# A vision tower on one core: own orders and two token banks in the last two steps, unread products in TensorE's waits, and an earlier first half of the tree

## The reference

```
tokens: patches of 1, 2 and 4 pixels along Hilbert curves, 16 to a group
        -> 256 tokens x 64 at each level (levels 2 and 3 interpolated to 256)
h = concat(levels) @ Wf.T + bf                              # 16 x 256 x 192
h = h + attention(layernorm(h))                             # 12 heads of 16, causal, softmax
all_logits = layernorm(h) @ weights_in.T                    # 21 nodes
walk a binary tree for 10 steps by the sign of the logit at the current node (index clipped to 20)
out = h + sum over the path of gelu(logit) * weights_out[node]
```

## Time and profile before

| | us |
|---|---|
| runs | 365.19, 367.33, 373.09 (median 367.33) |
| profiled execution, its own time | 369.12 |
| its span, first to last instruction | 367.1 |
| mean granted clock of TensorE, share of full | 0.902 |
| busy: PE, DVE, ACT, POOL | 302.2, 230.2, 191.6, 189.3 |

### The profile page before, as it was taken

The page is one execution under the profiler, slowest core; times in us unless marked ns, Lnnn a source line. Parts: engine busy times, 40 slices in busy tenths (PEclk is TensorE's granted clock), DMA queues, the critical chain, the costliest instruction groups (busy, mean ns, idle before and its releaser), DMA issues.

```text
span 367.1 us, 8188 instructions
## 1 busy us (share of the span) xinstructions
PE 302.2 (82%) x2684; PEld 225.3 (61%) x2684; DVE 230.2 (63%) x1135; ACT 191.6 (52%) x394; POOL 189.3 (52%) x410
## 2 busy tenths in 40 slices
PE   1943259899768498999999999999999979799663
PEld 1931028857657375777777777776677657576463
DVE  3000013235565857898889888898988883767872
ACT  1301002334453365865776586568657644568681
POOL 4777710000001047766866686686668663455642
PEclk9975557999996989999999999999999976999868
DMA  7611100020056044343654367353435622000018
GB/s 194 204 25 20 20 7 3 19 63 0 7 125 127 1 96 73 97 120 81 88 110 100 79 89 122 89 83 104 106 81 89 120 90 44 1 4 2 3 54 289
DMA packets 27633, 27.80 MB, mean 76 GB/s; under 512 B 6850, under 2 KB 27328, under 8 KB 27592
## 3 DMA queue, kind: packets, MB, share of 16 engines
q1 hardware_dynamic: 24472, 25.00, 31.1%
q0 software_dynamic: 1184, 1.58, 1.7%
q10 hardware_dynamic: 1936, 0.72, 0.9%
HBM read 4.86 MB, written 3.15 MB: 22 GB/s over the span
## 4 chain that ended last, share of the span: by engine, by line
PE 75%; issue 8%; DVE 6%; ACT 3%; DMA 3%; SPq 2%; POOL 1%; DVEq 0%; POOLq 0%; ACTq 0%
PE bank L1129 8%; PE bank L1306 7%; PE bank L1360 6%; PE bank L1338 6%; PE bank L1251 4%; PE bank L1302 4%; PE bank L1342 3%; PE bank L1270 3%; PE bank L1285 3%; PE bank L1287 3%; PE bank L1259 3%; PE bank L1230 3%; PE bank L1363 3%; PE bank L1242 2%; SPq L303 2%
## 5 line engine op out<-in xcount | busy, mean ns | idle before, releaser
L849 DVE CUSTOM_DVE_ANT_0 C<-bank,MASKV 128x256 bf16<-128x256 f32 (+1 forms) x384 | 112.6, 351 | 30.4 <-PE bank L1306 23.5
L569 ACT ACTIVATE PT<-bank 128x512 f32<-128x512 f32 x144 | 80.7, 606 | 52.8 <-PE bank L1338 48.8
L376 POOL TENSOR_SCALAR_AFFINE_SELECT PT<-PT 128x256 f32<-128x256 f32 x144 | 66.4, 474 | 0.0
L354 POOL TENSOR_TENSOR PART<-RES,PART 128x256 bf16<-128x256 f32 (+1 forms) x31 | 28.0, 904 | 62.0 <-ACT PART L563 62.0
L1129 PE MATMUL bank<-X,OH 128*128 128x192 f32 x128 | 31.3, 390 | 28.1 <-issue 20.1
L1129 PEld LDWEIGHTS bank<-X,OH 128*128 128x128 f32 x128 | 26.5, 231 | 31.7 <-issue 23.6
L372 POOL TENSOR_TENSOR CARRY<-CARRY 1x1 f32<-1x1 f32 x96 | 17.6, 184 | 54.1 <-ACT PT L569 54.0
L767 DVE TENSOR_SCALAR OH<-IR,IOTA 128x1024 f32<-128x1024 int32 x8 | 5.8, 751 | 53.0 <-remote 38.1
L349 POOL DMA_INDIRECT G<-x,I x32 | 30.7, 960 | 9.8 <-issue 9.8
L849 DVE DVE_READ_ACCUMULATOR2_ANT MX<- 128x1 f32 x384 | 31.9, 83 | 0.0
L1360 PE MATMUL bank<-PT,VA 128*32 128x256 f32 x384 | 30.9, 392 | 0.1
(11 more groups left out here) (167 smaller groups left out, 643.2 us busy)
## 6 DMA issues: line engine op xcount, KB each, us to landing
QS<-PART SPq DMA_DIRECT2D x72, 96.0 KB, 3.8
KS<-PART SPq DMA_DIRECT2D x72, 96.0 KB, 3.6
out<-HT SPq DMA_DIRECT2D x7, 384.0 KB, 3.5
KSL<-PART SPq DMA_DIRECT2D x24, 96.0 KB, 3.2
QSL<-PART SPq DMA_DIRECT2D x24, 96.0 KB, 3.6
X<-x SPq DMA_DIRECT2D x8, 96.0 KB
G<-x,I POOLq DMA_INDIRECT x34
IR<-ix1r SPq DMA_DIRECT2D x1, 512.0 KB
```

Source lines behind the costliest of these rows:

```text
L376: pool.affine_select(out=e, in_=e, compare_op=ALU.is_ge, fill=0.0, base=0, pattern=[[0, n], [1, P]], channel_multiplier=-1).then_inc(cut_o ...
L569: nc.scalar.activation(PT[:, v, :], BANK[T_BANK[(SU * par + v) % 2]][:, :], ACT.Exp, scale=SCALE).then_inc(exp_ok, 1)
L849: ins = nc.vector.tensor_tensor_reduce(JUNK[:, n:n + keys], bank[:, j * keys:(j + 1) * keys], MASKV[:, S - keys:S], 1.0, LOWEST, ALU.add, ...
```

## The change

- TensorE multiplies constants (`WP` by itself, 128x192 float32) into a bank that is about to be overwritten, and nobody reads the result: 10 such products ahead of the first step's wait, 10 ahead of `max_t(first)`, 3 ahead of the wait for the maxima in `scores_t` unit 0 of images 13, 14 and 15, 5 ahead of the last `project`, 1 and 2 around `tokens_t(15)`, 1 in each of `output(1)` to `output(4)`.
- Steps 14 and 15 get an order of their own on TensorE, ScalarE and VectorE (`closing_step`), and `tokens_t` alternates between banks 7 and 6. `project(12)` and `project(13)`, which use bank 6, wait for the copies.
- In the tail the logits are scaled for A and B apart (GpSimd), GELU of A and its coefficients come sooner, the remainders of A stand ahead of B's walk on GpSimd, its low parts still behind it; the GELU table for C is loaded ahead of `logits_t(7)`; VectorE copies `tokens_t(15)`; `coefficients_t(0)` and `(1)` stand around `logits(7)`, and `output(0)` follows at once; outputs take six banks in turn; GpSimd's output adds wait until C's coefficients are done.

```diff
-        OUT_BANK = [2, 3, 4, 6]
+        OUT_BANK = [2, 3, 4, 6, 5, 7]
...
-            return BANK[MB if i < 2 * 4 else S_BANK[i % 2]]
+            return BANK[(MB, MA)[i % 2] if i < 2 * 4 else S_BANK[i % 2]]
... GpSimd, tail
+            scaled(ROWS_A)
             pool.wait_ge(lgd_ok, 2)
-            pool.tensor_tensor(SL[:, ROWS_AB, :], LG[:, ROWS_AB, 0:NODES],
...
+            scaled(ROWS_B)
             normalise(Image(0, B - 1))
...
+            remainders(1, ROWS_A)
             pool.wait_ge(gn_ok, 2)
...
             low_parts(1, ROWS_A)
+            remainders(2, ROWS_B)
             low_parts(2, ROWS_B)
...
+            pool.wait_ge(co_ok, 3)
... ScalarE
+            def closing_step(b, par):
+                d, q = b - 1, 2 * (b.off - B + 2)
+                exp(d, 1 - par, 0)
+                tokens_t(2 * q)
+                exp(d, 1 - par, 1)
+                exp(d, 1 - par, 2)
+                exp(d, 1 - par, 3)
+                tokens_t(2 * q + 1)
+                exp(d, 1 - par, 4)
+                exp(d, 1 - par, 5)
+                logits_t(q)
+                tokens_t(2 * q + 2)
+                tokens_t(2 * q + 3)
+                exp(d, 1 - par, 6)
+                exp(d, 1 - par, 7)
+                exp(d, 1 - par, 8)
+                logits_back(q)
+                maxima(b)
+                logits_t(q + 1)
+                logits_back(q + 1)
...
-            gelu(1, ROWS_AB)
+            gelu(1, ROWS_A)
             tokens_t(14)
+            gelu(2, ROWS_B)
             logits_t(6)
             nc.scalar.activation(WARM[:, 0:1], WARM[:, 1:2], ACT.Sqrt)
             high_parts(ROWS_A)
-            tokens_t(15)
+            middle_parts(ROWS_A)
             deviations(5, ROWS_C)
-            middle_parts(ROWS_A)
+            nc.scalar.activation(WARM[:, 0:1], WARM[:, 1:2], ACT.Gelu)
             logits_t(7)
+            coefficients_t(0)
             high_parts(ROWS_B)
+            coefficients_t(1)
+            middle_parts(ROWS_B)
             gelu(3, ROWS_C)
-            middle_parts(ROWS_B)
-            coefficients_t(0)
-            coefficients_t(1)
             coefficients_t(2)
... VectorE
+            def closing_step(b, par):
+                d = b - 1
+                row_max(b, par, 0)
+                row_max(b, par, 1)
+                row_max(b, par, 2)
+                row_max(b, par, 3)
+                if b.late:
+                    centre()
+                row_max(b, par, 4)
+                row_max(b, par, 5)
+                row_max(b, par, 6)
+                heads_by_row(b - 2)
+                row_max(b, par, 7)
+                row_max(b, par, 8)
+                residual(b - 2)
+                heads_by_token(d, False)
+                residual_statistics(b - 2)
+                heads_by_token(d, True)
+                over_sums(d)
...
             residual(before)
+            own_rstd(4, ROWS_AB)
             copy_logits(5)
-            own_rstd(4, ROWS_AB)
             heads_by_token(last, False)
             heads_by_token(last, True)
             over_sums(last)
+            coefficients(1, ROWS_A)
+            heads_by_row(last)
             residual_statistics(before)
-            heads_by_row(last)
-            coefficients(1, ROWS_A)
             residual(last)
...
             variances(ROWS_C)
+            tokens_t(15)
             copy_logits(6)
...
+            output(0)
             for k in range(NQ):
-                if ADDED[k] == "dve":
+                if ADDED[k] == "dve" and k:
... TensorE
+            def keep_busy(bank, count):
+
+                for _ in range(count):
+                    nc.tensor.matmul(bank[:, 0:D], WP[:, 0, 0:P], WP[:, 0, :], start=True, stop=True)
...
                 if v == 0:
+                    if b.off >= B - 3:
+                        keep_busy(bank, 3)
                     pe.wait_ge(m_in, b.count(16, 16))
...
+            def closing_step(b, par):
+                d, q = b - 1, 2 * (b.off - B + 2)
+                for w in range(2):
+                    pe.wait_ge(stacked[w][par], 6 * 16 * (b.off // 2 + 1))
+                scores(b, par, 0)
+                scores(b, par, 1)
+                scores_t(d, 1 - par, 0)
+                tokens_t(2 * q)
+                if b.late:
+                    centre()
...
+                scores_t(d, 1 - par, 2)
+                tokens_t(2 * q + 1)
+                scores_t(d, 1 - par, 3)
+                scores(b, par, 4)
...
+                scores_t(d, 1 - par, 8)
+                project(b - 2)
+                weighted(d, 1 - par, 1)
+                max_t(b)
+                logits(q + 1)
+                weighted(d, 1 - par, 2)
+                logits_back(q + 1)
...
+                keep_busy(BANK[S_BANK[0]], 10)
                 for w in range(2):
                     pe.wait_ge(stacked[w][0], 6 * 16)
...
                 pe.wait_ge(ht_ok, B)
+                keep_busy(BANK[T_BANK[0]], 10)
                 max_t(first)
...
             logits(6)
+            pe.wait_ge(exp_ok, last.count(SU, SU))
+            keep_busy(BANK[T_BANK[0]], 5)
             project(last)
             logits_back(6)
+            keep_busy(BANK[T_BANK[0]], 1)
             tokens_t(15)
-            logits(7)
-            logits_back(7)
+            keep_busy(BANK[T_BANK[0]], 2)
...
+            coefficients_t(0)
+            logits(7)
+            coefficients_t(1)
+            logits_back(7)
             pe.wait_ge(w6_ok, 4 + PARTS)
-            for k in range(NQ):
+            output(0)
+            for k in range(2, NQ):
                 coefficients_t(k)
-                if k:
-                    output(k - 1)
+                output(k - 1)
             output(NQ - 1)
```

More of the change, by code:

```diff
@@ L687, in _ @@
             first_step()
[L688 removed]
+            for n in range(1, B - 2):
                 step(Image(0, n), n % 2)
+            for n in range(B - 2, B):
+                closing_step(Image(0, n), n % 2)
             last = Image(0, B - 1)
             def gelu(u, rows):
[L692 removed]
+                act.wait_ge(*((sl_ok, u) if u < 3 else (slc_ok, 1)))
                 nc.scalar.activation(GE[:, rows, :], SL[:, rows, :], ACT.Gelu).then_inc(ge_ok, 1)
@@ L916, in step @@
                 row_max(b, par, 0)
-                if b.late:
-                    centre()
                 if has_old:
@@ L1003, in _ @@
             first_step()
-            for n in range(1, B):
+            for n in range(1, B - 2):
                 step(Image(0, n), n % 2)
+            for n in range(B - 2, B):
+                closing_step(Image(0, n), n % 2)
             last = Image(0, B - 1)
@@ L1109, in _ @@
             last_reach(ROWS_B)
-            coefficients(1, ROWS_B)
+            coefficients(2, ROWS_B)
             own_rstd(5, ROWS_C)
@@ L1430, in step @@
                     narrow(f)
-                if b.late:
-                    centre()
                 scores_t(d, 1 - par, 0)
-                if closing:
-                    tokens_t(2 * q)
                 scores(b, par, 2)
```

98 lines of the change are left out of this document (49 added, 49 removed).

## The result

The changed kernel took 354.80 us in the median of four runs (354.23 to 355.40), beside 367.88 us for the kernel before. The ratio is 0.9668 (95% interval 0.9611 to 0.9726): 3.3% faster. The forecast was 356.5 us. The profiled execution took 354.23 us, with a span of 352.5 us and a mean granted clock of 0.943 (0.902 before).

What follows compares the result with a forecast made beforehand. TensorE was taken as the bound through the kernel's middle, losing time in waits and at half clock. Terms -2.6 - 1.5 - 1.5 - 5.0 - 2.5 + 0.3 = -12.8 us from 369.1 gave 356.3, stated as 356.5; range 351.5 to 364.

Steps and rivals of the forecast that it cites:

- the case that it called likeliest: Whole kernel: the forecast itself, 356.5 us, given a chance of 0.60.
- Part 1: Ahead of the first step: ten products fill the 4.24 us wait and hold the clock up, -2.6 us.
- Part 2: Ahead of `max_t(first)`: ten products fill the 4.16 us wait and keep the work behind it at full clock, -1.5 us.
- Part 3: Step 15: new order and second bank remove idle time, three products counted as 0.98 us of work, -1.5 us.
- Part 4: Step 14: same new order, with the 9.29 us at half clock now at full clock, -5.0 us.
- The sign of failing that I had named: Step 14: the prediction fails if the clock there is a matter of chance in both kernels.
- Part 5: Tail: five products ahead of the last `project`, earlier A coefficients and `output(0)`, -2.5 us.
- Part 6: Remaining products, around `tokens_t(15)`, in four outputs and ahead of the last image's scores: cost +0.3 us.
- The clock did not fall in the last two steps: Rival, steps 14 and 15: the clock falls all the same, giving back 4.65 us, 361; chance 0.15.
- the first step gave what it should: Rival, first step: it gives nothing, giving back 4.1 us, 360.5; chance 0.08.
- no product overran: Rival, all products: they run at low clock and overrun their waits, +10.6 us, whole kernel 376; chance 0.05.
- The tail's order loses: Rival, tail: collisions and late GpSimd adds make it 0.5 us slower instead of 2.5 faster, 359.5; chance 0.12.

Runs made afterwards that it cites:

- e2: Kernel before plus only the two groups of ten unread products (ahead of the first step and of `max_t(first)`): 364.07 us, ratio 0.9926.
- e1: Changed kernel without any of the unread products; orders, banks and tail rearrangement stay: 358.34 us, ratio 0.9741.
- e8: Kernel before plus only the second token bank, old orders of steps 14 and 15, no products: 361.44 us, ratio 0.9830.
- e3: Kernel before plus the own orders of steps 14 and 15 and the two token banks, no products, old tail: 360.67 us, ratio 0.9817.
- e7: Changed kernel with one token bank instead of two in steps 14 and 15; orders and products stay: 357.30 us, ratio 0.9756.
- e10: Changed kernel with VectorE's adds of `output(0)` moved ahead of C's walk: 323.89 us, ratio 0.9704 to the kernel before on the same chip.
- e13: The changed kernel run once more, unaltered, on another chip: 322.79 us, ratio 0.9645 to the kernel before there.
- e6: Kernel before plus both groups of ten products, two token banks and own orders of steps 14 and 15; old tail: 356.78 us, ratio 0.9739.
- e9: Changed kernel with `heads_by_row(last)` put back ahead of A's coefficients on VectorE: 356.84 us, ratio 0.9742.
- e4: Changed kernel without the three products ahead of the last image's transposed scores: 354.77 us, ratio 0.9648.
- e11: Changed kernel without GpSimd's wait for C's coefficients ahead of its output adds: 324.99 us, ratio 0.9742 to the kernel before on the same chip.

## Why the prediction was right, by its own steps

The forecast of 356.5 us was 1.7 us too high, and the case that it called likeliest came true. But the sum's agreement is better than its terms'.

**Part 1** (-2.6): right, -2.98. The reason holds too: the first step lost nearly the 3.05 us that half clock had cost, and e2 shows it alone. VectorE didn't become the bound there: of its four waits of 2.93 us in all one of 0.49 us is left. So the gain went to the end of the estimate.

**Part 2** (-1.5): too high. With the tens the way to step 2 is 1.1 us shorter in the change and 0.8 in e2. I wrote that there was room for 1.6 us, just. There wasn't: in all profiles with the tens TensorE stands idle ahead of step 2's first scores, 0.33 us in the change and 0.61 in e2, where the kernel before has no idle time. The profile names no releaser for it; in the program the wait for the stacked queries and keys stands there.

**Part 3, step 15** (-1.5): mis-sized, -2.7. The step has 12.10 us, all of it busy by the stretch's row, so the 0.3 us of idle time that I allowed aren't there. The other error is the 12.04 us of work, which I took as fixed: in e1 the same matmuls are busy 11.28 us of 12.18, and the rest is a wait of 0.90 us for the maxima. The triple stands in this wait and adds nothing. I had seen that it would cost nothing there and added its 0.98 us all the same. e8 shows that 1.6 of the 2.7 us are the bank's and e3 that 1.1 are the orders'.

**Part 4, step 14** (-5.0): size right, -5.7; the reason not as written. I put the full clock down to the triples and the denser order. e1 has no triples and e8 neither, and the clock stands in both; e7 keeps waits of 0.79 us and it stands too. In the profiles of kernels without second bank and without new orders (before and e2) it fell, and in none of the twelve others. But e8 shows the same work and the same waits ahead of the place, so for the bank alone this can't be read as cause and effect. The text said that the clock here may differ between executions and that the spread of the runs comes from it. The granted clocks of the single executions bear that out for the kernel before, on the chips of e10 to e13: spans of 330.2 to 330.7 us have a mean clock of 0.962 to 0.964, spans of 332.5 to 333.8 us 0.944 to 0.950, and spans of 334.5 us and more 0.945 or less.

Only one execution of each kernel has a trace, but the mean clocks allow an estimate: the missing share, doubled, times the span is the time at half clock. In the profile of the kernel before, the stretches around the first step and behind the fall in step 14 have

```profile
109.00:132.00 23.00, 15.14 (x80) 12.64 (x81) 14.32 (x96) 9.73 (x21) 4.96 (x7) 0.78 0.29 58
309.10:367.10 58.00, 42.74 (x498) 32.82 (x490) 37.69 (x140) 34.52 (x69) 29.64 (x66) 0.88 0.17 56
```

which is 10 and 14 us at half clock, and the fall in step 14 is 10 more. On the chips of e10 to e13 the front runs at 1.00 in all four traces, so an execution of the kernel before should have about 34 us with that fall and 24 without. Of its 18 executions there, 4 have 24 to 25 us and 14 have 33 to 41. The 20 executions of e10 to e13, which all have both banks and the new orders, have 4 to 11. By this estimate the kernel before loses the clock in step 14 in most executions, the change in none, so step 14 in the two profiles is what most executions have. The sign of failing that I had named, chance in both kernels, didn't come. But what decides it is not shown: which of bank and orders keeps the clock up, and why it stands or falls behind equal work. For the bank alone the times give a hint only. e8's median is 4.6 us under that of before (6.2 by the ratio). At any clock the bank takes 1.6 us off step 15 (14.82 to 13.24) and 0.4 off step 14 (18.56 less half of the 9.29 us at half clock is 13.9, against 13.51). That leaves 2.6 to 4.2 us for the clock, in step 14 or elsewhere.

**Part 5, the tail** (-2.5): the term that was mis-sized most, about 0 by the profiles (33.54 us before, 33.40 after; e6 with the old tail 33.33). My -2.5 was +0.4 for the way to `project`, -1.2 for `project` itself and -1.7 for what comes behind it. Measured are +1.3, -0.9 and -0.5. The -0.9 are there in e3, e6 and e8 as well (end 18.50 us), whose tail is the old one: the last `project` runs at the full clock in them, too. What I counted on for `output(0)` was there: it starts 3.4 us sooner behind `project`. What went wrong is this:

- The way to the last `project` grew by 1.3 us, and A's coefficients, to which I gave 0.6, are only 0.5 of it (e9). Another 0.4 came with the closing orders, for which I had no term: `max_t(15)` comes late in step 15, so the last image's transposed scores wait for the maxima's transfer (0.40 us in e1 and e3, which the kernel before doesn't have). And 0.4 are the last triple's (e4, Part 6). How A's coefficients cost their part: the two operations of GpSimd's `normalise` took 0.82 and 0.65 us, and VectorE's L1114 0.79 beside them; with `heads_by_row` first (e9) these are 0.62, 0.40 and 0.49. These are VectorE and GpSimd in the changed kernel:

```profile
327.43 0.26 DVE CO L1113
327.71 0.79 DVE CO L1114
```

```profile
327.33 0.82 POOL L398 TENSOR_TENSOR ON<-OB,RC 128x256 f32<-128x256 f32 x1 [0.82 <-DVE RC L907]
328.12 0.65 POOL L401 TENSOR_TENSOR ON<-OB,RC 128x128 f32<-128x128 f32 x1
```

(the first fence is the chain that ended last, the second GpSimd in time).

- The collisions were in my upper end, as two or three of 0.5 us. On VectorE they cost about what they cost before: 0.79, 0.33 and 0.61 us for operations that take 0.49, 0.20 and 0.17 elsewhere, where the kernel before had 0.74 and 0.51 us for 0.18 and 0.24.
- The head start of `output(0)` ends at a bank. I wrote that TensorE can do three outputs before VectorE frees one, and so it does, but VectorE's first add ends at 340.3, and the chain shows why: it runs through C's walk and coefficients on VectorE without a break.

```profile
333.31 0.68 DVE X2T L1071
...
337.83 0.40 DVE RE L1097
...
339.64 0.17 DVE CO L1119
339.82 0.47 DVE HT L1126
340.33 0.59 PE bank L1343 x2
```

C's coefficients end 10.2 us behind the start of `project` (before 10.7), of which 0.68 is the copy of `tokens_t(15)` now ahead of them. From there to the last add it is 7.8 us, before 8.7. In the kernel before the chain ran elsewhere: from B's coefficients over ScalarE, with the table load of 1.28 us, to `output(0)` on TensorE.

```profile
351.84 0.48 ACT COT L714
352.37 0.82 PE bank L1610 x4
```

The new order took this path away. But VectorE's path lay right behind it: its first adds of before follow C's coefficients without a wait.

```profile
353.31 1.01 DVE L1080 TENSOR_TENSOR HT<-bank,HT 128x384 f32<-128x384 f32 x2
```

So the 3.4 us of `output(0)` came down to 0.5. The step that failed is the -1.7 for the end: with the other path gone, VectorE's walk and coefficients of C are the bound.

The Trainium skill, "SBUF — State Buffer" ("Terms", shared port pair), has the later of VectorE and GpSimd wait for the whole of the other's instruction. The rows agree: L1110 in e11 started 0.03 us into GpSimd's first add of 0.98 us and took 1.06 us instead of 0.24, and the next took 1.04 beside the second add.

**Part 6** (+0.3): near. The last triple costs 0.4 us up to `project` and can't be told from nothing in the whole kernel. Without any product (e1) the clock is low in parts of the end, which then takes 18.34 us instead of 17.98.

**The rivals.** The clock did not fall in the last two steps; the first step gave what it should; no product overran, since ten took 3.42 us in the trace. "The tail's order loses" is the nearest to what happened, short of its price: I had the tail 0.5 us slower than now, and it came out level. Parts 3 and 4 gave 1.9 us more than forecast, which nearly made up for the tail; that the sum came out so close is luck in this respect: without the front's 2.2 us the profile has -12.4 us, where the sum had -12.8.

## What to carry to other kernels

A wait whose length and end the engine can't change is the cheap place for work that is read by nobody: ten products of 0.33 us in a wait of 4.2 us gave back 3.0 us of work at half clock, because they ended ahead of what the wait was for. Before a new order of a step is made, give the step another buffer and time that alone: here one more bank alone showed 6.6 of the 8.4 us in the profile, though only 2.0 of them are waits that it took away, and the rest hangs on a clock of which it isn't shown that the bank kept it up. And before the path that ends last is shortened (here ScalarE's table load ahead of `output(0)`), look at what ends next: here VectorE's chain lay right behind it, and of 3.4 us gained on the one path 0.5 came out.

## What the runs showed that I had not expected

**The front differs by 32 us between chips.** The runs came from four chips or more. On the two of e10 to e13 the first scores start near 78 us, on the others near 110, in code that no kernel here changes. The costliest groups show where. The change in its first profile:

```profile
L793 DVE TENSOR_SCALAR OH<-IR,IOTA 128x1024 f32<-128x1024 int32 x8 | 5.8, 751 | 50.9 <-remote 38.0
```

and e10:

```profile
L793 DVE TENSOR_SCALAR OH<-IR,IOTA 128x1024 f32<-128x1024 int32 x8 | 5.9, 758 | 19.8 <-PE bank L1177 15.3
```

VectorE's comparisons of the front were held for 38 us by something that the profile calls remote. In e10 this is missing. The change's ratio is 0.9668 where the kernel takes 367.9 us, and 0.9645 where it takes 335.5 (e13). The cause of the 38 us stays open. Among the profiles of the slow chips the first scores start between 107.6 and 112.9 us (e4 and e8), too, which is as large as many of the effects here.

**The clock fell without a reason that TensorE's own rows of this step show**, as told under e8: same matmuls, waits of 0.60 or 0.62 and 0.67 us, 2.54 us busy in 3.67, and the clock at half in one execution and at full in the other. In e1 it stood at full through a wait of 1.18 us in the same step.

**Step 1 varies by 0.6 us in kernels that agree up to there** (12.89 to 13.48 us with the tens), which is as much as most of the tail's edits were worth. All of it is the idle time ahead of step 2's first scores, 0.30 us in e4 and 0.89 in e7.
